# A gated Mamba and mixture-of-experts block on one core: gate folded into the output weights, residual made a sequence ahead, moments by aggregation, and a new slot table

## The chip, the cores and the metric

The kernel is one program on one core of a Trainium2 chip. The time is device microseconds of that core for one launch, as the median of repeated runs. A chip core has a matrix engine (TensorE, in the profile PE), a vector engine (VectorE, DVE), an activation engine (ScalarE, ACT), a general engine (GpSimd, POOL) and a queue engine (SyncE, SP), which here issues all transfers. Each engine takes its own instructions in the order of the program and waits on semaphores for the others.

## The reference, cut to what matters

```python
h = layernorm(x) * (1 + ca) + sa                # ca, sa, ga, cb, sb, gb: rows of silu(c) @ wmod, one per sequence
xn = (h - mean(h)) * rsqrt(var(h) + 1e-5) * norm_g + norm_b
x = x + ga * (h + mamba_fwd(xn) + mamba_bwd(xn))
h = layernorm(x) * (1 + cb) + sb
x = x + gb * moe(h)                             # 8 experts, top 2 by a router, and a shared one
# mamba: u, z = xn @ Win.T; u = silu(conv4(u)); dt = softplus(...); then for each of 16 states n
#   state = exp(dt*A[n]) * state + dt*u*B[n];  y += state*C[n]   (a scan over 512 tokens)
# y = (y + u*D) * silu(z);  result y @ Wout.T
```

Sixteen sequences of 512 tokens and 128 channels; the Mamba part has 256 inner channels (two halves of 128 partitions) and runs in both directions; every expert has 256 hidden channels. All is float32.

## The kernel before

There is a pass for each sequence `b`, and each pass has 32 **slots**: slots 0 to 15 are the 16 states of the forward scan, slots 16 to 31 those of the backward scan. Passes 2 to 14 are a hardware loop, the others are written out. Into the slots of pass `b` the kernel puts, engine by engine, the experts of sequence `b-1` (`ffn_side`, `expert_up`, `expert_silu`, `expert_sum`) and the preparation of the backward scan of `b` and of the forward scan of `b+1` (`prep`, with the slot offsets `U_AT` to `V_AT`, and `norms`). The tables of slots at the top of the file thus fix the order of every engine's queue; nothing is scheduled while the program runs.

In every slot the same five things happen. POOL makes `bt` (two halves at once) for the *next* slot (`bmul(step)`, which waits until the scan of two steps earlier is done: `bt` has two buffers). ACT makes the two halves of `psA = exp(dt*A)` for the next slot (`exps`), a half as soon as DVE has read that half of `psA` out. DVE scans both halves in place (`scan`) and multiplies them by C into `g` (`read_out`). PE adds `g` up in `psY` (`sum_y`).

Where the experts are up, a slot also has: two matmuls into `F0` and `F1` (`expert_up`), on ACT `tf` = tanh of `F0` and a copy `gf` of `F1`, on DVE in the following slot `pf` between the two read-outs, on POOL `act`; and on PE half of a down projection (`DOWN_SLOTS`), and after each second half on DVE a `facc` sum of four pieces. `up_at(slot)` and `down_at(slot)` turn a slot into a piece of expert work.

The chain to the experts of a sequence starts with the gated result of the Mamba part: the projection into `F2` (PE, `PROJ_SLOT` and the next), its sum with the kept `h` on DVE (`fx`, `FX_SLOT`), on POOL times the gate and plus a second copy of x (`x2`, two tensor operations), then layernorm (`LN3_SLOT`: four `BN_STATS` on DVE, `moments` on POOL, four activations `zF` on ACT), a transposition and the modulation into `h2T` (`H2T_SLOT`), the router's matmul (`GATE_SLOT`) and its small operations on DVE one slot later (`gate`), then `ge` (ACT), `gs` (POOL), `gw` (DVE) and `expert_weights` (POOL).

Softplus needs a logarithm, and twice in a pass (`ln1p`, in slots 9 and 28) ACT loads another table for it, and with the next function that isn't in that table it loads the first one back.

The order of parts within one slot of ACT's queue is this, and that of POOL is alike (`bmul`, `side`, `ffn_side`):

```python
exps(STEPS * b + nxt, b, nxt // N, nxt % N)   # for the next slot
ln1p(...)                                     # slots 9 and 28
s.activation(h1K, z1, ACT.Copy)               # one slot
ffn_side(b - 1, slot)                         # zF, h2T, ge, tf, gf, first facc
side(b, slot, True, b + 1)                    # norms and prep
```

Of the kernel before, what the change touches and what calls it, by code (L numbers as in the profile page):

```python
# [1163 lines left out]
```

## Time and profile before

| | us |
|---|---|
| median of 3 runs (2624.6 to 2626.51) | 2625.07 |
| the profiled execution | 2627.43 |
| its span, first to last instruction | 2625.6 |

The profiled execution took 2.36 us more than the median of the runs, and 1.83 us of it lie outside its span. Its mean granted TensorE clock is 0.897 of full speed. Times in rows are from the span's start. Two rows of one engine that follow each other overlap by some 0.05 to 0.09 us, so that what an instruction costs its queue is the distance of the starts.

### The profile page before, as it was taken

Reading aid. Unit: us, or ns where it says so; the run is one execution under the profiler, and the core shown is the slowest. Engines: PE = TensorE matmul, PEld = TensorE weight load, DVE = VectorE, ACT = ScalarE, POOL = GpSimd, SP = SyncE. Lnnn points to the kernel's source line nnn. Section 1 sums busy time; section 2 is a strip of 40 time slices with the busy share of each in tenths; the row PEclk is TensorE's granted clock in tenths of the full one; section 3 lists DMA queues with packets and bytes.
Section 4 is the critical chain, followed back from the end, with each engine's and each line's share of the span. In section 5 each row is a group of like instructions: output and inputs, shape, how many; then the busy total and the mean of one; then the engine's idle time right before and its main releaser. Section 6 shows DMA issues by size and latency. Waiting matters only on the chain. (4 is left out here: it accounts for less than half of the span.)

```text
span 2625.6 us, 37957 instructions
## 1 busy us (share of the span) xinstructions
PE 2125.2 (81%) x9893; PEld 1356.4 (52%) x9893; DVE 2288.6 (87%) x3603; ACT 1513.2 (58%) x2468; POOL 1958.1 (75%) x1437
## 2 busy tenths in 40 slices
PE   3677887978788797888889788787978879798868
PEld 1244554555555455555546555454555545455544
DVE  1699998989899898998989899898989989899973
ACT  2546656655565665656656565665556566565633
POOL 1577878778787877878777787877878787787854
PEclk6777998989899898998989899898989989899999
DMA  2334232333323233332333423333332333333320
GB/s 81 128 129 140 99 131 104 113 122 108 134 96 128 106 113 121 112 128 99 113 121 117 133 96 129 105 109 125 109 133 97 124 110 113 121 112 123 113 67 5
DMA packets 120494, 293.33 MB, mean 112 GB/s; under 512 B 18516, under 2 KB 53172, under 8 KB 120388
## 3 DMA queue, kind: packets, MB, share of 16 engines
q1 hardware_dynamic: 120388, 292.30, 33.0%
q14 instruction: 86, 0.70, 0.1%
q8 instruction: 20, 0.33, 0.0%
HBM read 285.91 MB, written 6.34 MB: 111 GB/s over the span
## 5 line engine op out<-in xcount | busy, mean ns | idle before, releaser
L426 POOL TENSOR_TENSOR bt<-v,bb 128x1024 f32<-128x1024 f32 x512 | 1207.1, 2361 | 178.2 <-DVE psA L783 175.7
L783 DVE TENSOR_TENSOR_SCAN psA<-psA,bt 128x512 f32<-128x512 f32 x1024 | 1198.0, 1216 | 126.1 <-POOL bt L426 90.9
L600 ACT ACTIVATE psA<-dt,aneg 128x512 f32<-128x512 f32 x1024 | 684.7, 688 | 745.1 <-DVE g L793 738.8
L983 PEld LDWEIGHTS psY<-ident,g 128*128 128x128 f32 x4096 | 517.4, 152 | 475.2 <-DVE g L793 267.7
L983 PE MATMUL psY<-ident,g 128*128 128x128 f32 x4096 | 606.9, 294 | 164.5 <-DVE g L793 164.4
L793 DVE TENSOR_TENSOR g<-psA,cb 128x512 f32<-128x512 f32 x1024 | 673.3, 677 | 0.0
L526 POOL TENSOR_TENSOR act<-pf,gf 128x512 f32<-128x512 f32 x288 | 366.2, 1272 | 256.5 <-DVE pf L878 224.9
L1064 PE MATMUL F<-h2T,w 128*128 128x512 f32 x576 | 337.2, 669 | 87.5 <-DVE pf L878 87.4
L1108 PE MATMUL F<-w,act 128*128 128x128 f32 x2304 | 319.4, 284 | 47.0 <-POOL act L526 43.4
L1108 PEld LDWEIGHTS F<-w,act 128*128 128x128 f32 x2304 | 291.6, 198 | 64.9 <-issue 57.9
L1067 PE MATMUL F<-h2T,w 128*128 128x512 f32 x576 | 308.3, 618 | 0.0
L878 DVE SCALAR_TENSOR_TENSOR pf<-tf,F 128x512 f32<-128x512 f32 x288 | 194.6, 676 | 73.0 <-ACT tf L693 73.0
L999 PE MATMUL psP<-xnT,wcT 128*128 128x512 f32 x512 | 248.8, 609 | 5.2 <-DVE zs L819 2.2
L693 ACT ACTIVATE tf<-F 128x512 f32<-128x512 f32 x288 | 169.7, 589 | 139.4 <-PE F L1064 138.9
L696 ACT ACTIVATE gf<-F 128x512 f32<-128x512 f32 x288 | 172.2, 598 | 73.1 <-PE F L1067 71.4
L1064 PEld LDWEIGHTS F<-h2T,w 128*128 128x128 f32 x576 | 97.8, 202 | 195.7 <-DVE pf L878 135.5
L1067 PEld LDWEIGHTS F<-h2T,w 128*128 128x128 f32 x576 | 116.8, 203 | 153.2 <-issue 152.6
L1015 PE MATMUL psP<-xnT,wzT 128*128 128x512 f32 x128 | 101.7, 888 | 91.3 <-DVE zs L819 87.6
L892 DVE SCALAR_TENSOR_TENSOR facc<-F,wts,facc 128x128 f32<-128x128 f32 x512 | 143.2, 343 | 10.7 <-PE F L1108 10.5
L999 PEld LDWEIGHTS psP<-xnT,wcT 128*128 128x128 f32 x512 | 90.8, 198 | 74.1 <-issue 65.8
L472 POOL TENSOR_TENSOR dt<-xb,ab 128x1024 f32<-128x1024 f32 x32 | 75.1, 2347 | 47.4 <-ACT ab L648 46.6
L1012 PE MATMUL psP<-xd,wdtT 8*128 8x512 f32 x128 | 93.5, 818 | 15.5 <-ACT xd L630 9.9
(134 smaller groups left out, 1730.1 us busy)
## 6 DMA issues: line engine op xcount, KB each, us to landing
bb<-bc_rows SPq DMA_DIRECT2D x256, 512.0 KB, 3.7
cb<-bc_rows SPq DMA_DIRECT2D x256, 512.0 KB, 3.6
x<-in_L_attn_x SPq DMA_DIRECT2D x16, 256.0 KB, 3.7
xR<-in_L_attn_x SPq DMA_DIRECT2D x16, 256.0 KB, 3.5
out_x<-osb SPq DMA_DIRECT2D x16, 256.0 KB, 3.9
w<-in_L_ffn_ew SPq DMA_DIRECT2D x2, 1024.0 KB
modA<-mod_table SPq DMA_DIRECT2D x16, 128.0 KB, 3.9
bc_rows<-xd SPq DMA_DIRECT2D x32, 64.0 KB, 2.8
```

The lines of the kernel that those rows point to most:

```text
L426: g.tensor_tensor(bt[:, n % 2, :, :], v[d][:, :, :], bb[:, n // 2 % 2, n % 2, :].unsqueeze(1).broadcast_to([P, NH, T]), ALU.mult).then_inc ...
L526: g.tensor_tensor(act[:, k // 2 % 3, k % 2, :], pf[:, k % 2, :], gf[:, k % 3, :], ALU.mult)\
L600: s.activation(psA[:, half * T:half * T + T], dt_[d][:, half, :], ACT.Exp, scale=aneg[d][:, half, n:n + 1]).then_inc(a_s, 1)
L696: s.activation(gf[:, k % 3, :], F1[:, :], ACT.Copy).then_inc(F1_free, 1)
L783: w.tensor_tensor_scan(ah, ah, bt[:, n % 2, half, :][:, order], 0.0, ALU.mult, ALU.add)\
L793: w.tensor_tensor(g_[:, n % 2, half, :], psA[:, half * T:half * T + T], cb[:, n // 2 % 2, n % 2, :], ALU.mult).then_inc(g_s, 1)
L878: w.scalar_tensor_tensor(pf[:, k % 2, :], tf[:, k % 2, :], 1.0, F0[:, :], ALU.add, ALU.mult).then_inc(pf_s, 1)
L983: last = m.matmul(psY[:, half * T + i * P:half * T + i * P + P], g_[:, n % 2, half, i * P:i * P + P], ident[:, :], is_transpose=True, star ...
L999: last = m.matmul(psP[:, :], wcT[d][:, half, j, :], xnT[:, lo:lo + T], start=(j == 0), stop=(j == TAPS - 1))
L1064: m.matmul(F0[:, :], w1[:, x_, half * P:half * P + P], h2T[:, :], start=True, stop=True)\
L1067: m.matmul(F1[:, :], w2[:, x_, half * P:half * P + P], h2T[:, :], start=True, stop=True)\
L1108: last = m.matmul(F2[:, i * D:i * D + D], act[:, e % 3, half, i * P:i * P + P], w3[:, ORDER[e], half, :], start=(half == 0), stop=(half == 1))
```

## The change

**The gate is folded into the output weights.** POOL multiplies both directions' output weights by the gate's row once per pass (`wg`, in `WG_SLOT` = 2), and PE projects with `wg`. The residual and the gated `h` are added ahead: `hx = h*ga + x` is made on POOL in slot 23 of the pass before, copied on ACT (`hxK`), and DVE adds it to the projection, which gives `x2` at once. POOL's two operations on `x2` and the second load of x (`xR`) fall away, `modA` has a third row, and the next load of x waits for `hx` and not for `h1`.

**Moments by aggregation.** After the four `BN_STATS` DVE waits for them, clears four numbers and does four `BN_AGGR`; POOL's `moments` has four operations in place of eight.

**A table load of its own** follows each logarithm (`preload_act_table`).

**New slots.** First norm's statistics 9 to 8, its moments 10 to 9, `z1` 11 to 10; Z pieces a slot later; `x2` 5 to 4 and its statistics in the same slot (6 before), its moments 6 to 5, `zF` 7 to 5, the transposition 8 to 6 and behind the other work of PE's slot, router 9 to 7, its small operations 10 to 8, `ge` and `gs` 11 to 9, expert weights 13 to 11. The experts' up slots begin at 7 (9 before) and leave out 9, 10 and 22; the down slots begin at 10 (12 before) and leave out 12, 13, 20 and 23.

```diff
-U_AT, XD_AT, DT_AT, LN1P_AT, Z_AT, V_AT = 0, 6, 7, 9, 9, 11
-LN_SLOT, XN_SLOT = 9, 16
+U_AT, XD_AT, DT_AT, LN1P_AT, Z_AT, V_AT = 0, 6, 7, 9, 10, 11
+STAT_SLOT, RSTD_SLOT, Z1_SLOT, H1_SLOT, STAT2_SLOT, RSTD2_SLOT, XNORM_SLOT, XN_SLOT, HX_SLOT = 8, 9, 10, 12, 13, 14, 15, 16, 23
-POSTB_SLOT, PROJ_SLOT, FX_SLOT, LN3_SLOT, H2T_SLOT, GATE_SLOT = 1, 3, 5, 6, 8, 9
+POSTB_SLOT, WG_SLOT, PROJ_SLOT, X2_SLOT, LN3_SLOT, H2T_SLOT, GATE_SLOT = 1, 2, 3, 4, 4, 6, 7
-UP_SLOTS = [slot for slot in range(9, 28) if slot not in (22,)]
-DOWN_SLOTS = [slot for slot in range(12, 32) if slot not in (19, 21)]
+UP_SLOTS = [slot for slot in range(7, 28) if slot not in (9, 10, 22)]
+DOWN_SLOTS = [slot for slot in range(10, 32) if slot not in (12, 13, 20, 23)]
...
-                wait(sp, h1_s, 2 * b)
+                wait(sp, hx_s, 2 * b)
...
-                row = mod_dram[bass.ds(b, 1), 0:2 * D].broadcast_to([P, 2 * D])
+                row = mod_dram[bass.ds(b, 1), 0:3 * D].broadcast_to([P, 3 * D])
...
-                    sp.dma_start(xR[:, :, :], t["x"][bass.ds(fb, 1)].rearrange("a (k p) d -> p (a k) d", p=P))\
-                        .then_inc(xR_in, 16)
...
-                g.tensor_tensor(stat_[:, :, 0:2], st_[:, :, 1:3], st_[:, :, 4:6], ALU.add).then_inc(sig, 1)
-                g.tensor_tensor(stat_[:, :, 2:3], st_[:, :, 1:2], st_[:, :, 4:5], ALU.subtract).then_inc(sig, 1)
+                g.tensor_tensor(stat_[:, :, 2], stat_[:, :, 1], epsilon[:, :], ALU.add).then_inc(sig, 1)
+                g.tensor_tensor(stat_[:, :, 3], stat_[:, :, 0], negative[:, :], ALU.mult).then_inc(sig, 1)
                 pool.wait_ge(sig, q + 2)
-
-                g.tensor_tensor(stat_[:, :, 0:3], stat_[:, :, 0:3], scales[:, :, :], ALU.mult).then_inc(sig, 1)
+                g.tensor_tensor(rstd_[:, :], stat_[:, :, 2], mhalf[:, :], ALU.pow).then_inc(sig, 1)
                 pool.wait_ge(sig, q + 3)
...
+                g.tensor_tensor(stat_[:, :, 4], stat_[:, :, 3], rstd_[:, :], ALU.mult).then_inc(sig, 1)
...
+                if slot == HX_SLOT:
+
+                    wait(pool, hxK_s, b)
+                    g.tensor_tensor(hx[:, :, :], z1[:, :, :], over_tiles(modA[:, 2, :]), ALU.mult).then_inc(hx_s, 1)
+                    pool.wait_ge(hx_s, 2 * b + 1)
+                    g.tensor_tensor(hx[:, :, :], hx[:, :, :], x[:, :, :], ALU.add).then_inc(hx_s, 1)
...
-                if slot == FX_SLOT:
-                    pool.wait_ge(F2_free, (DOWN + 1) * fb + PROJ + 1)
+                if slot == WG_SLOT:
                     pool.wait_ge(modF_in, 48 * fb + 48)
-                    wait(pool, o_s, 2 * fb)
-                    g.tensor_tensor(x2[:, :, :], fx[:, :, :], over_tiles(modF[:, 0, :]), ALU.mult).then_inc(x2_s, 1)
-                    pool.wait_ge(x2_s, 2 * fb + 1)
-                    pool.wait_ge(xR_in, 16 * fb + 16)
-                    g.tensor_tensor(x2[:, :, :], x2[:, :, :], xR[:, :, :], ALU.add).then_inc(x2_s, 1)
...
+                    wait(pool, F2_full, (DOWN + NE) * (fb - 1) + PROJ + 1)
+                    g.tensor_tensor(wg[:, :, :, :].rearrange("p a k d -> p (a k) d"),
+                                    wout_both[:, :, :, :].rearrange("p a k d -> p (a k) d"),
+                                    over_tiles(modF[:, 0, :]), ALU.mult).then_inc(wg_s, 1)
...
                 s.activation(ab[:, :, :], ab[:, :, :], ACT.Ln, bias=1.0).then_inc(sp_s, 1)
+                s.preload_act_table(ACT.Exp)
...
-                        if slot == FX_SLOT + 2:
+                        if slot == X2_SLOT + 2:
...
-                            s.activation(h1K[:, :, :], z1[:, :, :], ACT.Copy).then_inc(h1K_s, 1)
+                            s.activation(hxK[:, :, :], hx[:, :, :], ACT.Copy).then_inc(hxK_s, 1)
...
                 for i in range(NT):
                     w.bn_stats(st_[:, i, :], x_[:, i, :]).then_inc(sig, 1)
+                dve.wait_ge(sig, q + NT)
+                w.memset(stat_[:, :, 4], 0.0)
+                for i in range(NT):
+                    w.bn_aggr(stat_[:, i, 0:2], st_[:, i, :]).then_inc(sig, 1)
...
-                    w.tensor_tensor(fx[:, :, :], F2[:, :].rearrange("p (k c) -> p k c", c=D), h1K[:, :, :], ALU.add)\
+                    w.tensor_tensor(x2[:, :, :], F2[:, :].rearrange("p (k c) -> p k c", c=D), hxK[:, :, :], ALU.add)\
                         .then_inc(F2_free, 1)
...
+                        pe.wait_ge(wg_s, fb + 1)
...
-                                            woutT[k // NH][:, k % NH, :], start=(k == 0), stop=(k == 2 * NH - 1))
+                                            wg[:, k // NH, k % NH, :], start=(k == 0), stop=(k == 2 * NH - 1))
```

**ACT, slot 9.** Before the change, ACT's queue in the loop has here the second half of the exponentials for slot 10 (`psA`), the logarithm behind its table load (L648), and then the load that belongs to the first tanh of the experts, `tf`:

```order
L600 ACTIVATE psA<-dt,aneg 128x512
L647 REGISTER_ALU
L648 ACT_TABLE_LOAD
L648 ACTIVATE ab<-ab 128x1024
L691 ISA
L273 REGISTER_ALU
L693 ACT_TABLE_LOAD
L693 ACTIVATE tf<-F 128x512
L273 REGISTER_ALU
L696 ACTIVATE gf<-F 128x512
```

After the change the same place reads:

```order
L593 ACTIVATE psA<-dt,aneg 128x512
L640 REGISTER_ALU
L641 ACT_TABLE_LOAD
L641 ACTIVATE ab<-ab 128x1024
L642 ACT_TABLE_LOAD
L680 REGISTER_ALU
L681 ACTIVATE ge<-gd 128x4
L275 ISA
L593 ACTIVATE psA<-dt,aneg 128x512
```

The load back stands directly behind the logarithm (L642), `tf` has left the slot, and the router's exponential `ge` (L681) now stands behind both loads; before, it stood in slot 11.

**POOL, slots 9 to 11.** Before the change POOL's queue around `gs`, the operation that needs `ge`, is this; the `bt` ahead of `v` is the one for slot 11, made in POOL's slot 10, with `gs` in its slot 11:

```order
L472 TENSOR_TENSOR dt<-xb,ab 128x1024
L522 ISA
L273 REGISTER_ALU
L526 TENSOR_TENSOR act<-pf,gf 128x512
L273 ISA
L426 TENSOR_TENSOR bt<-v,bb 128x1024
L475 REGISTER_ALU
L273 ISA
L477 TENSOR_TENSOR v<-u,dt 128x1024
L504 TENSOR_TENSOR gs<-ge,ones 128x4
```

After the change:

```order
L436 TENSOR_TENSOR stat<-stat,rstd 128x4
L499 TENSOR_TENSOR gs<-ge,ones 128x4
L515 REGISTER_ALU
L519 TENSOR_TENSOR act<-pf,gf 128x512
L275 ISA
L424 TENSOR_TENSOR bt<-v,bb 128x1024
L465 ISA
L466 ISA
L467 TENSOR_TENSOR dt<-xb,ab 128x1024
L275 ISA
L424 TENSOR_TENSOR bt<-v,bb 128x1024
```

`gs` has moved two slots forward, and what stands behind it now is the second `act` of the experts, the `bt` of slot 11 (the first `bt` of this piece), `dt` and the `bt` of slot 12.

**DVE, slots 4 and 5.** Before the change, the slot of the projection's sum is slot 5, and its statistics come a slot later:

```order
L793 TENSOR_TENSOR g<-psA,cb 128x512 x2
L812 REGISTER_ALU
L819 SCALAR_TENSOR_TENSOR u<-th,psP 128x512
L900 REGISTER_ALU
L273 REGISTER_ALU
L903 TENSOR_TENSOR fx<-F,h1K 128x512
L779 REGISTER_ALU
L781 ISA
```

After the change, slot 4 has:

```order
L787 TENSOR_TENSOR g<-psA,cb 128x512 x2
L898 REGISTER_ALU
L275 REGISTER_ALU
L901 TENSOR_TENSOR x<-F,hxK 128x512
L904 ISA
L275 REGISTER_ALU
L793 BN_STATS stF<-x 128x6 x4
L794 ISA
L795 MEMSET statF 128x4
L797 BN_AGGR statF<-stF 128x2 x4
```

The sum, here written to x2 (`x` in the row), its statistics and the aggregation now stand together in slot 4, behind the read-outs `g`.

## Rows read from the trace of the kernel before

**Rows 1.** The page's part 1: engine, busy us, share, instructions.

```profile
PE 2125.2 (81%) x9893; PEld 1356.4 (52%) x9893; DVE 2288.6 (87%) x3603; ACT 1513.2 (58%) x2468; POOL 1958.1 (75%) x1437
```

**Rows 2.** Timeline of DVE from slot 4: start, us, instruction, [idle before <-releaser].

```profile
1165.68 2.35 DVE L783 TENSOR_TENSOR_SCAN psA<-psA,bt 128x512 f32<-128x512 f32 x2 [0.17 <-ACT psA L600]
...
1169.36 2.35 DVE L783 TENSOR_TENSOR_SCAN psA<-psA,bt 128x512 f32<-128x512 f32 x2 [0.16 <-ACT psA L600]
...
1174.00 2.34 DVE L783 TENSOR_TENSOR_SCAN psA<-psA,bt 128x512 f32<-128x512 f32 x2
...
1177.43 0.86 DVE L799 BATCH_NORM_STATS2 stF<-x 128x6 f32<-128x128 f32 x4
1179.46 2.35 DVE L783 TENSOR_TENSOR_SCAN psA<-psA,bt 128x512 f32<-128x512 f32 x2 [1.17 <-POOL bt L426]
...
1184.64 2.35 DVE L783 TENSOR_TENSOR_SCAN psA<-psA,bt 128x512 f32<-128x512 f32 x2 [1.65 <-POOL bt L426]
```

**Rows 3.** Timeline of DVE, slots 10, 11 and the start of 16.

```profile
1198.20 0.69 DVE L878 SCALAR_TENSOR_TENSOR pf<-tf,F 128x512 f32<-128x512 f32 x1 [2.75 <-ACT tf L693]
...
1200.33 0.36 DVE L849 MAX8 top<-gl 128x8 f32<-128x8 f32 x4
...
1202.01 2.35 DVE L783 TENSOR_TENSOR_SCAN psA<-psA,bt 128x512 f32<-128x512 f32 x2
...
1228.04 1.23 DVE L783 TENSOR_TENSOR_SCAN psA<-psA,bt 128x512 f32<-128x512 f32 x1 [0.90 <-POOL bt L426]
```

**Rows 4.** Timeline of ACT, slot 9.

```profile
1191.29 1.30 ACT L600 ACTIVATE psA<-dt,aneg 128x512 f32<-128x512 f32 x2
1192.61 1.28 ACT L648 ACT_TABLE_LOAD   x1
1193.90 1.06 ACT L648 ACTIVATE ab<-ab 128x1024 f32<-128x1024 f32 x1
1196.19 1.28 ACT L693 ACT_TABLE_LOAD   x1 [1.23 <-PE F L1064]
```

**Rows 5.** Timeline of POOL, layernorm moments in slot 6.

```profile
1179.29 0.21 POOL L433 TENSOR_TENSOR statF<-stF 128x8 f32<-128x8 f32 x1
...
1180.88 1.02 POOL L445 TENSOR_TENSOR rstdF<-statF,mhalf 128x4 f32<-128x4 f32 x1
...
1182.14 2.37 POOL L426 TENSOR_TENSOR bt<-v,bb 128x1024 f32<-128x1024 f32 x1
```

**Rows 6.** Timeline of POOL, slots 11 to 13.

```profile
1207.06 0.20 POOL L504 TENSOR_TENSOR gs<-ge,ones 128x4 f32<-128x4 f32 x1 [2.12 <-ACT ge L687]
...
1208.46 2.37 POOL L426 TENSOR_TENSOR bt<-v,bb 128x1024 f32<-128x1024 f32 x1
1210.78 1.28 POOL L461 TENSOR_TENSOR xn<-z,modA 128x512 f32<-128x512 f32 x1
...
1216.93 0.19 POOL L492 TENSOR_TENSOR gw<-gw,ge 128x4 f32<-128x4 f32 x1
```

**Rows 7.** Timeline of SP, the gate's rows being fetched.

```profile
1158.55 0.38 SPq L383 DMA_DIRECT2D modC<-mod_table  x1
```

**Rows 8.** DMA issues: KB each, median us from issue to landing.

```profile
modC<-mod_table SPq DMA_DIRECT2D x16, 1.0 KB, 3.4
```

**Rows 9.** Timeline of PE, projection in slots 3 and 4.

```profile
1162.14 2.05 PE L1081 MATMUL F<-woutT,acc 128*128 128x128 f32 x16 [0.54 <-DVE acc L837]
...
1166.62 1.95 PE L1081 MATMUL F<-woutT,acc 128*128 128x128 f32 x16
```

**Rows 10.** Timeline of PE, first and second pair into F0.

```profile
1194.19 1.90 PE L1064 MATMUL F<-h2T,w 128*128 128x512 f32 x2
...
1201.10 1.02 PE L1064 MATMUL F<-h2T,w 128*128 128x512 f32 x2
```

**Rows 11.** Busy times in one stretch: length, engines, PEclk, DMA share, GB/s.

```profile
1178.90:1192.30 13.40, 10.29 (x32) 6.46 (x33) 11.02 (x15) 9.74 (x18) 11.35 (x13) 0.50 0.33 123
```

**Rows 12.** Timeline of DVE, slot 29.

```profile
1293.70 0.69 DVE L819 SCALAR_TENSOR_TENSOR zs<-th,psP 128x512 f32<-128x512 f32 x1 [1.37 <-ACT th L621]
```

More of the change, by code:

```diff
@@ L98, in adaln_mamba_moe @@
         wdtT = [sb(f"wdtT{d}", [R, NH, P]) for d in range(2)]
-        woutT = [sb(f"woutT{d}", [P, NH, D]) for d in range(2)]
+        wout_both = sb("woutT", [P, 2, NH, D])
+        woutT = [wout_both[:, d, :, :] for d in range(2)]
         norm = sb("norm", [P, 2])
@@ L111, in adaln_mamba_moe @@
         gabs = sb("gabs", [NB, 2, D])
-        modA = sb("modA", [P, 2, D])
+        modA = sb("modA", [P, 3, D])
         modF = sb("modF", [P, 2, D])
@@ L222, in adaln_mamba_moe @@
         h1_s = sem("h1_s")
-        h1K_s = sem("h1K_s")
+        hx_s = sem("hx_s")
+        hxK_s = sem("hxK_s")
+        wg_s = sem("wg_s")
         pP_full = sem("pP_full")
@@ L412, in _ @@
             g.memset(ones[:, :], 1.0).then_inc(const_ok, 1)
-            for k, scale in enumerate((-0.5, 1.0 / D, 0.5)):
-                g.memset(scales[:, :, k:k + 1], scale).then_inc(const_ok, 1)
+            g.memset(negative[:, :], -1.0).then_inc(const_ok, 1)
             def over_tiles(row):
@@ L463, in norms @@
                     g.tensor_tensor(z1[:, :, :], xn[:, :, :], over_tiles(modA[:, 0, :]), ALU.add).then_inc(h1_s, 1)
-                if slot == LN_SLOT + 5:
-                    pool.wait_ge(lnA, 8 * b + 8)
-                    moments(st, stat, rstd, rstdA, 16 * b + 8)
+                if slot == HX_SLOT:
[3 more added lines that the diff above has]
+                    g.tensor_tensor(hx[:, :, :], hx[:, :, :], x[:, :, :], ALU.add).then_inc(hx_s, 1)
+                if slot == RSTD2_SLOT:
+                    pool.wait_ge(lnA, 16 * b + 16)
+                    moments(stat, rstd, rstdA, 8 * b + 4)
             def make_dt(b, d):
@@ L898, in ffn_side @@
                     gate_y(fb, 1, slot - POSTB_SLOT)
-                if slot == FX_SLOT:
+                if slot == X2_SLOT:
                     dve.wait_ge(F2_full, (DOWN + NE) * fb + PROJ + 1)
-                    dve.wait_ge(h1K_s, fb + 1)
+                    dve.wait_ge(hxK_s, fb + 1)
                     wait(dve, o_s, 2 * fb)
-                    w.tensor_tensor(fx[:, :, :], F2[:, :].rearrange("p (k c) -> p k c", c=D), h1K[:, :, :], ALU.add)\
+                    w.tensor_tensor(x2[:, :, :], F2[:, :].rearrange("p (k c) -> p k c", c=D), hxK[:, :, :], ALU.add)\
                         .then_inc(F2_free, 1)
                 if slot == LN3_SLOT:
-                    dve.wait_ge(x2_s, 2 * fb + 2)
-                    wait(dve, rstdF_s, 8 * fb)
-                    statistics(x2, stF, lnF)
+                    dve.wait_ge(F2_free, (DOWN + 1) * fb + PROJ + 1)
+                    wait(dve, rstdF_s, 4 * fb)
+                    statistics(x2, stF, statF, lnF, 8 * fb)
                 if slot == GATE_SLOT + 1:
@@ L1056, in expert_up @@
                 free = (DOWN + 1) * fb
+                if slot == H2T_SLOT:
+                    pe.wait_ge(zF_s, NT * fb + NT)
+                    pe.wait_ge(F2_free, free + H2T)
+                    for i in range(NT):
+                        last = m.transpose(F2[:, i * P:i * P + P], zF[:, i, :], ident[:, :])
+                    last.then_inc(F2_full, 1)
                 k = up_at(slot)
@@ L1081, in ffn_late @@
                             last = m.matmul(F2[:, i * D:i * D + D], yg[k // NH][:, k % NH, i * P:i * P + P],
-                                            woutT[k // NH][:, k % NH, :], start=(k == 0), stop=(k == 2 * NH - 1))
+                                            wg[:, k // NH, k % NH, :], start=(k == 0), stop=(k == 2 * NH - 1))
                     if slot == PROJ_SLOT + 1:
                         last.then_inc(F2_full, 1)
-                if slot == H2T_SLOT:
-                    pe.wait_ge(zF_s, NT * fb + NT)
-                    pe.wait_ge(F2_free, free + H2T)
-                    for i in range(NT):
-                        last = m.transpose(F2[:, i * P:i * P + P], zF[:, i, :], ident[:, :])
-                    last.then_inc(F2_full, 1)
                 if slot == GATE_SLOT:
```

68 lines of the change are left out of this document (29 added, 39 removed).

## Prediction

> **What bounds the kernel now.** The page comes first: DVE is busy for 87% of the span [rows 1], more than any other engine, so the question in each place is what DVE waits for. I then read DVE's timeline over one pass of the loop, a slot at a time, from the scan of slot 4 at 1165.68 to that of slot 16 at 1228.04 [rows 2, 3]: 62.36 us. The reader is to see three kinds of slot. A bare one takes 3.68 us, of which some 0.2 is a wait for the exponentials (1165.68 to 1169.36). One with a further 128x512 operation hides that wait: slot 5 has two, `u` and `fx`, and takes 4.64. I take 3.45 for the scans and read-outs alone and 0.60 for each addition. The third kind waits for something else: 1.17 and 1.65 us for `bt` at the starts of slots 7 and 8 [rows 2], 2.75 for `tf` in slot 10, 0.90 for `bt` at the start of slot 16 [rows 3]. The first two are the `x2` chain on POOL. The 2.75 is ACT's: a logarithm behind a table load, a wait for `F0`, a second load [rows 4].
>
> **From slot 4 to DVE's first read-out of slot 9.** I call the end of that read-out T, since ACT's exponentials for slot 10 start there. Before, slot 9 starts 3.68+4.64+5.46+5.18+3.68 = 22.64 after slot 4 (the slots' lengths in rows 2; the last is a bare one), and scans and a read-out take 2.85, so T is at 25.5. The edits move it so:
> - `x2` now follows in slot 4 directly on the projection, which waits for `wg`, and `wg` for the gate's rows. These are issued at 1158.55 and land 3.4 later [rows 7, 8], at 1162.0, and a 128x512 operation on POOL takes 1.28 [rows 6]: PE starts near 1163.4, not 1162.14 [rows 9]. PE is busy from there to the end of the second part (1166.62+1.95 = 1168.57), so that ends near 1169.8, some 0.6 behind DVE's read-outs (1165.68+3.45): +0.6. POOL stands for these rows with the `bt` of slot 4 behind it; it ends at 1163.3+2.37 = 1165.7, just in time, cost nothing, and if a transfer takes 1 us longer, 1 us.
> - `fx` and `x2` are one operation either way; 0.
> - Aggregation is in no row. The bounds: four small operations in 0.36 us [MAX8, rows 3] below, four BN_STATS in 0.86 [rows 2] above. A BN_AGGR reads six numbers, so it is nearest MAX8. With the clearing and a wait for its own statistics I take 0.45, twice before T: +0.9 (0.7 to 1.9).
> - The statistics of x come into slot 8 from slot 9, where they stood behind T: +0.8 [0.86 less an overlap, rows 2].
> - The router's small operations come into slot 8 from slot 10: from 0.33 before MAX8 at 1200.33 to 1202.01 [rows 3], +2.0.
> - The first `pf` comes into slot 8: +0.6.
> - The waits for `bt` at slots 7 and 8 go, since POOL has nothing more to do to `x2`: -2.95 (with what surrounds them in the slot's lengths). Moments take POOL 2.85 us [rows 5]; with four of the small operations gone, at some 0.28 each, 1.75. They lie under slots that POOL has room in.
>
> The sum is +1.95, T at 27.4, if `tf` is there in time. Now the clock. Here the granted clock is 0.50, the 1.2 GHz level, for 13.4 us [rows 11], after slots in which PE had little to do, and a pair into `F0` takes 1.90 in place of 1.02 [rows 10]. I count the new chain: `x2` summed near 4.7 after slot 4's start, statistics to 5.9, moments to 7.7, exponentials, `zF` by 11.9, transposition to 13.4, `h2T` to 15.5, then router, a DT piece and the pair into `F0`: `tf` ends near 19.0 at the 2.4 GHz level, in time for the read-out at 20.2; at the 1.2 GHz level each of the three takes 0.9 more, `tf` ends near 21.7, and DVE waits 1.6. The gf, DT and second pair behind it then make ACT late for the exponentials of slot 10 by another 0.8. The stretch lies where the clock is low now, and its gaps on PE are much the same, so I take the low level: T is in effect at 29.8.
>
> **From T to the scan of slot 16.** In slot 9 `ge` now stands behind two table loads and the logarithm. The second half of the exponentials ends at T+1.9. Load, logarithm, load take 1.29+1.08+1.28 = 3.65 [rows 4], `ge` some 0.25: `gs` starts on POOL at T+5.9. It and `act` take 1.40 [1207.06 to 1208.46, rows 6], and only then does POOL make the `bt` of slot 11, 2.31 long: the scan of slot 11 starts at T+9.8. Free of this it would be T+1.2+3.7 = T+4.9. So the wait for `tf`, 2.75, is gone and one of 4.9 for `bt` takes its place. What is queued behind on POOL is not hidden either, as these slots have the most POOL work of the pass. From T+9.6: `dt` 2.3, `bt` 2.3, `v` 2.3, expert weights 1.0 (five small ones), `bt` 2.3, then the two of the modulation, `act` and `bt` 6.15 [1210.78 to 1216.93, rows 6], `act` and `bt` 3.55, moments 1.75, `act` and `bt` 3.55: T+34.8. The last slot being DVE's own, the scan of slot 16 starts at T+35.2.
>
> So slot 16 starts at 65.0 (62.6 if the clock holds), against 62.36 before.
>
> ACT's exponentials end at 1192.59 and the load starts at 1192.61, the logarithm 0.01 after the load's end [rows 4]: a switch costs its 1.28 and nothing else. The Trainium skill (ScalarE: Activation LUTs, "What ACT_TABLE_LOAD costs") says that a switch of table costs 1283 ns and then about 1380 ns of draining. The load's duration agrees with the row, the drain doesn't. By the row load, logarithm and load take 3.65; by the skill's figure they would take 6.4 and `ge` come 2.8 later.
>
> **From slot 16 to the next slot 4.** The down slots shift by one, so that `facc` leaves slot 23, which has no `pf` and where it hid the wait for exponentials: +0.25. In slot 29 the wait of 1.37 for a tanh behind the table load [rows 12] goes, as Z comes a slot later; the exponentials of slot 30 now start behind both loads and cost 0.6: -0.8. `hx` on POOL in slot 23 is two operations of 1.28 [rows 6] in a slot without `act`, after slots in which POOL waits for DVE; 0, and if that room is gone, up to 2.5. The third row of `modA` and the missing load of x concern transfers that have a pass's time; 0. Together -0.55.
>
> **Sum.** A pass of the loop: 65.0-62.36-0.55 = +2.1. Fifteen passes have both experts and scans: +31. The ends: in the last pass `x2` loses POOL's two operations (2.6) and moments 1.1, and gains 0.45; the first passes lose moments twice and a tanh ahead of the logarithm, some 2.5: -6 in all. 2627.4+25 = 2652 for a profiled execution, whose time now is 2.4 above the median: 2650.
>
> **The rivals.**
> - *PE's clock holds through slots 6 to 8* (the case on the other side). For it: PE is busy almost without a gap from the transposition on, where before it waited. Against it: 13.4 us at 0.50 in the same slots now [rows 11]. Price: 2.4 us a pass less, a pass at -0.3, the whole 2627.4-5-6, as a median 2614. It decides at `tf`: ready before DVE's first read-out of slot 8, or not.
> - *The clock is low again after slot 9.* PE has only `sum_y` to do while POOL waits for `ge`. If it stays low until the third pair into `F0`, behind the down projection, Z and `sum_y`, `pf` in slot 12 waits up to 3 us: +45, 2695. Against it: DVE is late there too, and I count some 0.3 us in hand even with part of it low.
> - *POOL isn't held by `ge`.* Then the 4.9 goes and with it the queue behind, some 6.5 a pass: 2650-97 = 2553. Against it stands the order of both queues; nothing in the rows speaks for it.
> - *The second load drains ACT first.* Nothing stands between the logarithm and the load now, where before ACT waited for `F0`; if the load back had to wait for the logarithm's results as long as that runs, 1.06 [rows 4], and the first load for the exponentials likewise, `ge` and all behind it came 2.1 later: times 15, 2682. Against it stands the first load, directly behind the exponentials. By the Trainium skill's figure for the drain (ScalarE: Activation LUTs, the same section) it would be 2692.
>
> **How the numbers follow.** Forecast (low clock in slots 6 to 8, held by `ge`): 0.58, its own range 2632 to 2672 from aggregation up to 0.5 each dearer and the exponentials 0 to 1.7 late. Clock holds: 0.20. Low again: 0.12. Not held: 0.08. Drain: 0.02. The range of 2606 to 2688 leaves out "not held" and most of "low again". Within 0.2% (5 us, about what a measurement of this kernel can tell from no change): 0.12, half from the forecast's low end and half from the clock's. Faster 0.24: 0.08, 0.14 of the clock's and 0.02 of the forecast's. Slower 0.64.
>
> **What would show it.** In the profile after: `psA` in slot 11 waiting 4 to 5 us for `bt`, that `bt` behind `gs`, and `gs` waiting for `ge`; ACT with load, logarithm and load in one piece of 3.65; no `bt` wait at slots 7 and 8; four BN_AGGR within 0.3 to 0.5; PE's first projection waiting for `wg`; `pf` in slot 8 waiting 1.6 for `tf` with the granted clock at 0.50. If that clock stands at 1.00 there, or the wait at slot 11 is under 3 us, the forecast is too high; if PE is at 0.50 through slots 10 to 12 and `pf` waits in slot 12, too low.

## The result, and the profile after

The changed kernel takes 2667.16 us (median of 4 runs, 2662.65 to 2671.37), beside 2625.28 us for the kernel before on the same chip: a ratio of 1.0158, 95% interval 1.0145 to 1.0172. It is slower by 1.6%, 17 us above the predicted 2650 and inside the range. The profiled execution took 2671.37 us, 43.94 more than the one of before. One execution of the first experiment below (8637.84 us) and one of the second (3090.94) were slow ones; the medians given there include them, the ratios don't.

The page's part 1 (busy us, share, instructions) and groups of its part 5:

```profile
PE 2119.8 (79%) x9893; PEld 1351.9 (51%) x9893; DVE 2309.6 (87%) x3843; ACT 1508.7 (57%) x2468; POOL 1936.3 (73%) x1259
...
L777 DVE TENSOR_TENSOR_SCAN psA<-psA,bt 128x512 f32<-128x512 f32 x1024 | 1198.7, 1217 | 164.8 <-POOL bt L424 86.3
...
L890 DVE SCALAR_TENSOR_TENSOR facc<-F,wts,facc 128x128 f32<-128x128 f32 x512 | 143.6, 346 | 26.0 <-PE F L1107 26.0
```

DVE is busy 21 us longer than in [rows 1], with 240 more instructions: the clearing and the aggregation. The rest is waiting. The page's totals don't say where, so the timeline is read again, slot by slot. This is DVE in one pass, from slot 8 to slot 12:

```profile
1198.06 0.68 DVE L876 SCALAR_TENSOR_TENSOR pf<-tf,F 128x512 f32<-128x512 f32 x1
...
1199.25 0.86 DVE L793 BATCH_NORM_STATS2 st<-x 128x6 f32<-128x128 f32 x4
1200.16 0.17 DVE L797 BATCH_NORM_AGGREGATE stat<-st 128x2 f32<-128x6 f32 x1
1200.19 0.06 DVE L795 MEMSET stat<- 128x4 f32 x1
1200.25 0.28 DVE L797 BATCH_NORM_AGGREGATE stat<-st 128x2 f32<-128x6 f32 x3
1200.45 0.16 DVE L843 COPY gl<-F 128x32 f32<-128x32 f32 x1
...
1202.43 2.35 DVE L777 TENSOR_TENSOR_SCAN psA<-psA,bt 128x512 f32<-128x512 f32 x2
...
1211.56 0.18 DVE L867 RECIPROCAL gw<-gs 128x4 f32<-128x4 f32 x1 [1.25 <-POOL gs L499]
1215.20 2.34 DVE L777 TENSOR_TENSOR_SCAN psA<-psA,bt 128x512 f32<-128x512 f32 x2 [3.47 <-POOL bt L424]
```

ACT in slot 9 and 10, and POOL behind it:

```profile
1207.38 1.28 ACT L641 ACT_TABLE_LOAD   x1
1208.67 1.06 ACT L641 ACTIVATE ab<-ab 128x1024 f32<-128x1024 f32 x1
1209.75 1.28 ACT L642 ACT_TABLE_LOAD   x1
1211.04 0.21 ACT L681 ACTIVATE ge<-gd 128x4 f32<-128x4 f32 x1
```
```profile
1211.32 0.20 POOL L499 TENSOR_TENSOR gs<-ge,ones 128x4 f32<-128x4 f32 x1 [7.18 <-ACT ge L681]
1211.50 1.26 POOL L519 TENSOR_TENSOR act<-pf,gf 128x512 f32<-128x512 f32 x1
1212.72 2.36 POOL L424 TENSOR_TENSOR bt<-v,bb 128x1024 f32<-128x1024 f32 x1
```

The hold is there as forecast: `ge` behind load, logarithm and load, `gs` behind `ge`, `act` and `bt` behind `gs`, and DVE idle for 1.25 and then 3.47, together 4.72 us. In [rows 3] the same stretch has 2.75 for `tf`, which is gone: `pf` at 1198.06 follows its read-out directly. What wasn't forecast is at the end of the pass. PE first, then DVE, from slot 30 to the next pass's slot 0:

```profile
1311.97 2.08 PE L1013 MATMUL psP<-xnT,wzT 128*128 128x512 f32 x2 [3.38 <-DVE zs L817]
1313.83 1.91 PE L981 MATMUL psY<-ident,g 128*128 128x128 f32 x8
1315.54 1.64 PE L1107 MATMUL F<-w,act 128*128 128x128 f32 x8
```
```profile
1317.32 1.13 DVE L890 SCALAR_TENSOR_TENSOR facc<-F,wts,facc 128x128 f32<-128x128 f32 x4 [1.38 <-PE F L1107]
1320.50 2.35 DVE L777 TENSOR_TENSOR_SCAN psA<-psA,bt 128x512 f32<-128x512 f32 x2 [2.06 <-issue]
```

The kernel before, DVE in the same place:

```profile
1302.80 1.12 DVE L892 SCALAR_TENSOR_TENSOR facc<-F,wts,facc 128x128 f32<-128x128 f32 x4
1305.08 2.35 DVE L783 TENSOR_TENSOR_SCAN psA<-psA,bt 128x512 f32<-128x512 f32 x2 [1.17 <-POOL bt L426]
```

A piece of Z now stands in slot 30. It waits 3.38 us for `zs`, PE does nothing meanwhile, and Z, `sum_y` and the last down projection then run near the 1.2 GHz level (2.08 for a pair that took 1.02 elsewhere; the granted clock is the third number from the end of this row, behind the busy times of the engines):

```profile
1310.00:1317.00 7.00, 5.03 (x18) 3.89 (x19) 5.94 (x9) 3.21 (x5) 6.83 (x4) 0.52 0.29 95
```

`facc` waits 1.38 for them, and the next pass's first scan starts 2.06 after `facc`, a stretch for which the trace names no releaser. In the kernel before, the same piece stands one slot earlier and has the same wait, but there a whole slot lies between it and the last `facc`, which doesn't wait:

```profile
1294.44 1.63 PE L1015 MATMUL psP<-xnT,wzT 128*128 128x512 f32 x2 [3.82 <-DVE zs L819]
```

I measured the slots of the 13 passes of the loop from the third on and took means, in us (the starts of the scans in DVE's timeline):

| stretch | before | after | difference | forecast |
|---|---|---|---|---|
| scan of slot 0 to slot 4 | 16.42 | 16.67 | +0.25 | in the -0.55 |
| slot 4 to slot 16 | 62.40 | 63.12 | +0.72 | +2.6 |
| slot 16 to slot 31 | 71.32 | 70.42 | -0.90 | in the -0.55 |
| slot 31 to the next slot 0 | 5.72 | 8.45 | +2.73 | 0 |
| a pass | 155.85 | 158.66 | +2.81 | +2.1 |

The 2.73 at the end of a pass are three things: the addition `zs`, which now stands in slot 31 (0.6), the wait of `facc` (0.96 in the mean, 0 before) and a longer idle stretch ahead of slot 0's scan (2.25 for 1.17). That stretch comes with the loop's way back: the passes before the loop end without one, and so does the thirteenth, behind which the program goes straight on into a written-out one; there slot 31 to slot 0 takes 4.5 before and 5.8 after.

The thirteen make 36.4 of the 43.94. The pass before them has +3.1, the last one with scans +8.5, and the rest (start, first pass, tail) -3.6+0.75-1.1 = -4.0: together 44.0.

### The profile page after: what moved, and what is told of

It is laid out like the page before. It is cut to its first block and busy times, and to the rows that moved or that the text cites. A ratio compares the mean times of both kernels' runs of the same rounds, so it can differ in the third digit from the quotient of the medians.

```text
span 2669.6 us, 37830 instructions
## 1 busy us (share of the span) xinstructions
PE 2119.8 (79%) x9893; PEld 1351.9 (51%) x9893; DVE 2309.6 (87%) x3843; ACT 1508.7 (57%) x2468; POOL 1936.3 (73%) x1259
## 5 line engine op out<-in xcount | busy, mean ns | idle before, releaser
L981 PEld LDWEIGHTS psY<-ident,g 128*128 128x128 f32 x4096 | 524.0, 153 | 448.6 <-DVE g L787 224.9
L1068 PE MATMUL F<-h2T,w 128*128 128x512 f32 x576 | 335.0, 665 | 105.9 <-DVE pf L876 104.4
L1107 PE MATMUL F<-w,act 128*128 128x128 f32 x2304 | 329.1, 289 | 106.8 <-POOL act L519 99.7
L1107 PEld LDWEIGHTS F<-w,act 128*128 128x128 f32 x2304 | 301.6, 204 | 122.9 <-issue 95.0
L1071 PE MATMUL F<-h2T,w 128*128 128x512 f32 x576 | 317.4, 635 | 0.0
L1013 PE MATMUL psP<-xnT,wzT 128*128 128x512 f32 x128 | 100.0, 875 | 64.2 <-DVE zs L817 62.7
L614 ACT ACTIVATE th<-psP 128x512 f32<-128x512 f32 x128 | 76.2, 596 | 77.9 <-PE psP L1013 75.8
```

Of the source, the lines that this page charges most:

```text
L981: last = m.matmul(psY[:, half * T + i * P:half * T + i * P + P], g_[:, n % 2, half, i * P:i * P + P], ident[:, :], is_transpose=True, star ...
L1068: m.matmul(F0[:, :], w1[:, x_, half * P:half * P + P], h2T[:, :], start=True, stop=True)\
L1071: m.matmul(F1[:, :], w2[:, x_, half * P:half * P + P], h2T[:, :], start=True, stop=True)\
L1107: last = m.matmul(F2[:, i * D:i * D + D], act[:, e % 3, half, i * P:i * P + P], w3[:, ORDER[e], half, :], start=(half == 0), stop=(half == 1))
```

## The experiments

All ratios are to the kernel before, run on the same chip. Places are given by slots, since each kernel runs at its own times.

**`ge` ahead of the loads.** The computation is unchanged; ACT issues `ge` in slot 9 before the first table load.

```diff
-                if slot == GATE_SLOT + 2:
-                    act_e.wait_ge(gate_s, GATES * fb + GATE_D)
-                    s.activation(ge[:, :], gd[:, :], ACT.Exp).then_inc(ge_s, 1)
...
+                    if ffn and slot == GATE_SLOT + 2:
+                        act_e.wait_ge(gate_s, GATES * (b - 1) + GATE_D)
+                        s.activation(ge[:, :], gd[:, :], ACT.Exp).then_inc(ge_s, 1)
```

> The changed kernel with one thing moved: in ACT's slot 9 the router's exponential ge stands ahead of the logarithm and its two table loads, not behind them. Theory (POOL is held by ge): gs starts some 3.6 us earlier, the wait of 3.5 us for bt at the start of slot 11 falls to under 1 us, and what is queued behind on POOL comes as much earlier; about 3.5 us a pass, so about 2613 us. Rival (the loss is spread over aggregation, fold and the start of a pass, and POOL's hold is made good by slack later): under 1 us a pass, above 2650 us.

Measured: 2608.37 us, 0.9935 (0.9915 to 0.9955), 5 us below what the theory had. ACT and the scan of slot 11:

```profile
1185.03 0.19 ACT L713 ACTIVATE ge<-gd 128x4 f32<-128x4 f32 x1
1185.24 1.28 ACT L641 ACT_TABLE_LOAD   x1
```
```profile
1189.63 2.35 DVE L777 TENSOR_TENSOR_SCAN psA<-psA,bt 128x512 f32<-128x512 f32 x2 [1.75 <-ACT psA L593]
```

The releaser changes from POOL's `bt` to ACT's exponentials, which the loads hold in either kernel, and 1.75 is left of 4.72. Slot 4 to slot 16 takes 59.24 in place of 63.12. The one edit is worth 59 us of the whole: the hold is the largest single cost of the change, and it comes from the order of two things on ACT.

**`ge` two slots later.** `ge` and `gs` in slot 11, the reciprocal in 12, the weights in 13, so that no one waits for `ge`.

```diff
-                if slot == GATE_SLOT + 2:
+                if slot == GATE_SLOT + 4:
```

> The changed kernel with the router's tail back where it was: ge and gs in slot 11, gw in 12, expert weights in 13 (9, 9, 10, 11 in the changed kernel). Theory (POOL is held): the hold goes altogether, and what is left at the start of slot 11 is a wait for ACT's exponentials behind both loads, some 1.7 us; 2600 to 2615 us. Rival (spread): above 2650 us.

Measured: 2624.51 us, 0.9994 (0.9981 to 1.0008), 10 to 25 us above what was expected. Slot 11 has no wait for `bt`, but slot 12 has new ones. PE, DVE and the granted clock (PEclk) there:

```profile
1198.59 2.08 PE L1013 MATMUL psP<-xnT,wzT 128*128 128x512 f32 x2 [4.27 <-DVE zs L817]
1200.45 1.57 PE L1068 MATMUL F<-h2T,w 128*128 128x512 f32 x2
```
```profile
1202.69 0.69 DVE L876 SCALAR_TENSOR_TENSOR pf<-tf,F 128x512 f32<-128x512 f32 x1 [1.32 <-ACT tf L687]
```
```profile
1194.00:1198.00 4.00, 0.32 (x3) 0.12 (x2) 3.58 (x5) 3.67 (x8) 4.00 (x3) 1.00 0.26 95
1198.00:1204.00 6.00, 5.41 (x15) 2.89 (x16) 4.66 (x6) 2.48 (x7) 5.92 (x5) 0.72 0.45 152
```

PE has 0.32 us of work in 4 us, and then runs at 0.72 of its clock. Slot 12 takes 7.27 in the mean of the thirteen passes, 5.63 in the changed kernel, and five of them have a long slot 9, where the changed kernel has three. This is the rival "low again after slot 9": it exists, in a kernel where DVE is early enough to meet it. In the changed kernel `pf` in slot 12 waits in none of the thirteen passes; that DVE, held by `bt`, simply comes later there than PE is my reading of the rows.

**The old slots, the rest of the change kept** (the gate folded into the weights, aggregation, the extra preload; U and Z, norms, router and experts where they stood before; only the statistics of `x2` stand a slot earlier than then, in slot 5 behind the sum):

```diff
-U_AT, XD_AT, DT_AT, LN1P_AT, Z_AT, V_AT = 0, 6, 7, 9, 10, 11
+U_AT, XD_AT, DT_AT, LN1P_AT, Z_AT, V_AT = 0, 6, 7, 9, 9, 11
-POSTB_SLOT, WG_SLOT, PROJ_SLOT, X2_SLOT, LN3_SLOT, H2T_SLOT, GATE_SLOT = 1, 2, 3, 4, 4, 6, 7
+POSTB_SLOT, WG_SLOT, PROJ_SLOT, X2_SLOT, LN3_SLOT, H2T_SLOT, GATE_SLOT = 1, 2, 3, 5, 5, 8, 9
...
```

> Fold, residual ahead, aggregation and the extra table load as changed, but with the slots of before (x2 in slot 5 with its statistics behind it, transposition 8, router 9, experts up from 9, down from 12, Z as before). Theory (the slots cost, the rest gains): the bt waits at slots 7 and 8 are gone (-2.9 us a pass), the wait for tf is 1.3 us shorter, aggregation costs up to 1.35: 2580 to 2600 us. Rival (the fold and aggregation themselves cost): above 2625 us.

Measured: 2600.11 us, 0.9901 (0.9885 to 0.9918), the upper end of what the theory gave.

**Aggregation alone, in the kernel before** (statistics closed by BN_AGGR on DVE, four small operations fewer on POOL):

```diff
+                dve.wait_ge(sig, q + NT)
+                w.memset(stat_[:, :, 4], 0.0)
+                for i in range(NT):
+                    w.bn_aggr(stat_[:, i, 0:2], st_[:, i, :]).then_inc(sig, 1)
```

> The kernel before with aggregation alone: after each four BN_STATS DVE waits, clears and does four BN_AGGR, POOL's moments have four operations in place of eight. Theory (aggregation is cheap, 0.45 us each, and POOL's shorter moments pay for it where DVE waits for bt): 2600 to 2625 us. On the start of a pass in the loop: if DVE's longer loop body is what makes the idle time before slot 0 longer (1.2 us before, 2.3 after the change), it is above 2 us here too; if it is the late down projection or Z's shift, it stays at 1.2 us. Rival (aggregation costs 1 us each or more): above 2640 us.

Measured: 2608.65 us, 0.9934 (0.9918 to 0.9951). So aggregation alone makes the kernel 16 us faster. The folded gate, with what comes along with it, gives another 9, and the new slots cost 67. The 9 can't be put down to the gate alone: the preload is in that difference too. Here the load back waits 1.2 to 1.5 us for `F0`; in the old slots with the preload it waits for nothing, and the wait for `tf` is 2.05 in place of the 2.60 here. No run parts the two.

```profile
1180.65 2.35 DVE L771 TENSOR_TENSOR_SCAN psA<-psA,bt 128x512 f32<-128x512 f32 x2 [1.10 <-ACT psA L588]
...
1190.77 0.69 DVE L870 SCALAR_TENSOR_TENSOR pf<-tf,F 128x512 f32<-128x512 f32 x1 [2.60 <-ACT tf L681]
```

The two kernels take 5.68 and 5.65 from slot 31 to slot 0, as before, so the 2.73 at the end of the pass comes with the new slots, and not with the number of instructions in the loop.

**Z of the forward direction back a slot, in the changed kernel.** The piece in slot 30 then stands in slot 29.

```diff
-                if k - Z_AT in (0, 1):
-                    open_piece(Z, k - Z_AT)
+                if k - Z_AT + (d == 0) in (0, 1):
+                    open_piece(Z, k - Z_AT + (d == 0))
...
```

> The changed kernel with the two Z pieces of the forward preparation back in slots 28 and 29 (their sums on DVE in 29 and 30); those of the backward one stay. Theory: the late Z piece is what makes the end of a loop pass dear. PE stands for the sum of slot 30, its next down projection comes late, facc waits in slot 31, and the branch back, which otherwise starts while DVE still works, starts late too. Then slot 31 to the next slot 0 goes back from 8.45 to 5.7 us, slot 29 costs 1.5 more again: about -1.2 us a pass, 2649 us. Rival (DVE's longer loop body or the other edits make the branch back dear): slot 31 stays above 7.5 us and the kernel at 2665 us or above.

Measured: 2666.32 us, 1.0156 (1.014 to 1.0173): no gain where 18 us were expected. The end of the pass does what the theory says: 5.77 from slot 31 to slot 0 (2.68 less) and 6.53 in slot 29 (1.54 more, [rows 12]). But slot 4 to slot 16 takes 64.28, 1.16 more: `x2` waits 1.0 for PE in slot 4 in the mean (0.3 in the changed kernel), and 6 of the 13 passes have a long slot 9 (5.8 to 5.9), where the changed kernel has 3. One of the four passes with the long wait for `x2`, PE and DVE:

```profile
385.15 3.40 PE L1086 MATMUL F<-wg,acc 128*128 128x128 f32 x16 [2.04 <-POOL wg L505]
```
```profile
393.33 0.69 DVE L901 TENSOR_TENSOR x<-F,hxK 128x512 f32<-128x512 f32 x1 [2.36 <-PE F L1086]
```

The first half of the projection takes 3.40 here, at a granted clock of 0.65, and 2.02 at 1.00 in the pass behind it, where `x2` waits 0.32. PE has stood 2 us for `wg` before it, since POOL waits some 4 us for the gate's rows in every pass. So the cause of the 2.73 is shown, and the saving is given back in stretches that no edit touched, where the granted clock falls at other moments.

**PE kept busy in slot 30.** Three further matmuls ahead of that piece of Z, into F0, whose results nothing reads.

```diff
+                if d == 0 and k == Z_AT + 1:
+                    wait(pe, pf_s, 2 * NE * (b - 1))
+                    for _ in range(3):
+                        m.matmul(F0[:, :], wzT[d][:, 0, :], xnT[:, PAD:PAD + T], start=True, stop=True)
```

> The changed kernel with three matmuls more (128x512, into F0, which nobody reads then) on PE in slot 30, where it stands for DVE's sum. They compute nothing that is used. Theory (a low clock makes the down projection late): the granted clock stays at 1.00 there, the wait of facc in slot 31 falls from 1.0 us to under 0.3, and the time from slot 31 to slot 0 from 8.45 to some 7.3 us: 2650 us. Rival (the order of PE's queue alone makes it late): the wait stays at 1.0 us or grows, 2667 us or more.

Measured: 2649.34 us, 1.0098 (1.0079 to 1.0117), as expected: more work on PE takes 18 us away. The four executions lie between 2639.85 and 2655.72, and the profiled one is the fastest of them. PE, DVE and the clock:

```profile
1296.24 2.74 PE L1014 MATMUL F<-xnT,wzT 128*128 128x512 f32 x6
1299.78 1.13 PE L1017 MATMUL psP<-xnT,wzT 128*128 128x512 f32 x2 [0.80 <-DVE zs L817]
```
```profile
1303.67 1.12 DVE L890 SCALAR_TENSOR_TENSOR facc<-F,wts,facc 128x128 f32<-128x128 f32 x4
1306.55 2.35 DVE L777 TENSOR_TENSOR_SCAN psA<-psA,bt 128x512 f32<-128x512 f32 x2 [1.75 <-issue]
```
```profile
1298.00:1305.00 7.00, 6.20 (x32) 3.84 (x31) 6.79 (x12) 4.20 (x7) 6.83 (x4) 1.00 0.30 105
```

Z takes 1.13 in place of 2.08, the clock is 1.00, and `facc` no longer waits. Slot 31 to slot 0 is 6.55. So 1.9 of the 2.73 is PE at its lower level. Of the other 0.8, 0.6 is `zs`, which still stands in slot 31, and 0.2 stays in the stretch before slot 0's scan (1.41 in the mean, 1.17 in the kernel before); the cause of this last piece is open.

**Both, `ge` first and Z back.**

> Both single edits together: ge ahead of the logarithm, and the forward Z pieces back. If the two losses lie apart they add up: 2608 us less some 18, 2590 us. If the queue of POOL takes back what the end of the pass gives: 2605 us.

Measured: 2605.62 us, 0.9915 (0.9888 to 0.9942). Beside 2608.37 for `ge` first alone: the two don't add up, and the time is the 2605 that was given for that case. The end of the pass takes 2.9 less than with `ge` first alone, slots 16 to 31 take 1.7 more (nearly all of it slot 29), slots 4 to 16 0.7 more.

**The extra table load taken out** of the changed kernel (the preload that stands behind each logarithm):

```diff
-                s.preload_act_table(ACT.Exp)
```

> The changed kernel without the extra table load behind the logarithm: the load back then comes with ge in slot 9 and with the exponentials in slot 29. Theory (the load back is needed at the same place either way): within 5 us of the changed kernel, 2662 to 2672 us. Rival (the extra load costs or hides something of its own): more than 10 us away.

Measured: 2673.72 us, 1.0177 (1.016 to 1.0194), 6.6 us more than the changed kernel, whose interval it touches, and 1.7 above the expected stretch; a pass takes 158.61 for 158.66, with the same waits. The preload adds no load: every one of these kernels has 65 of them. Whether it is asked for or comes by itself with the next exponential makes next to no difference in these slots, so asking for it isn't what costs in the hold, its place ahead of `ge` is.

**PE kept busy in slots 5 and 7** of the changed kernel (three and one such matmuls), to lift the clock before the first pair into F0.

> The changed kernel with four matmuls more on PE (128x512, into F0, which nobody reads then, nothing used): three at the end of slot 5, where PE stands for DVE, and one in slot 7 after the sum. In the changed kernel 3 of the 13 loop passes lose some 1.8 us more in slot 9 than the others, with the clock at the lower level near 33 us into the pass, and the last pass with scans loses 4.3 us there. Theory (that is the clock): these go, worth 0.5 us a pass and 3 to 4 us once: 2653 to 2660 us. Rival (the order of the queues makes them, not the clock): 2665 us or more, as PE only has more to do.

Measured: 2665.46 us, 1.0157 (1.0118 to 1.0196), where 2653 to 2660 was expected. In the profiled execution the long slot 9 is gone from all 13 passes (4.04 to 4.54), slot 9 is 0.37 shorter in the mean, and the last pass with scans is 3.7 shorter, all as expected; but the second pass is 1.9 longer and what follows the last scans 3.7. The four executions spread from 2658.11 to 2679.54, so four can't show or rule out a gain of 5 us. And it isn't certain that the edit does what it is for: with the same matmuls in the next run, two of thirteen passes have a long slot 9 again.

**`ge` first, with PE kept busy** in slots 30, 5 and 7:

> ge ahead of the logarithm, and the fillers of both places (three matmuls in slot 30, three in slot 5, one in slot 7). The sum of the single edits: 2608 less 18 for slot 30 and less some 8 for the early ones: 2580 to 2590 us. If the fillers hold up something else once POOL is free: 2605 us.

Measured: 2593.38 us, 0.9876 (0.9857 to 0.9894), 3 us above the expected stretch. It is the fastest of all: 34 us below the kernel before on its chip and 74 below the changed one. A pass takes 153.5, slot 4 to slot 16 59.10, slot 31 to slot 0 6.96. Two passes have a slot 9 of 5.76 and 5.89, the granted clock being 0.78 in the 7.2 us from slot 7 of the first of them on.

**The old slots, with PE kept busy** in slots 5 to 8 (seven such matmuls):

```diff
+                        fill(b - 1, {5: 2, 6: 2, 7: 2}.get(slot, 0))
...
+                        fill(b - 1, {8: 1}.get(slot, 0))
```

> Fold, residual ahead and aggregation with the slots of before, and fillers on PE in slots 5, 6 and 7 (two each, at the end) and 8 (one). With the slots of before PE is at the lower level through slots 7 to 10, and DVE waits 2.0 us for tf in slot 10. Theory (the clock makes tf late): the wait falls to under 1 us; 2600 us less 15 to 25. Rival (the logarithm and its load on ACT make tf late, PE's pair was there in time): the wait stays above 1.5 us and the kernel at 2597 to 2603 us.

Measured: 2630.68 us, 1.0012 (1.0002 to 1.0022): 30 us more than without them, where 15 to 25 less was expected. PE, ACT and DVE around slot 9:

```profile
1342.49 3.78 PE L1056 MATMUL F<-xnT,wzT 128*128 128x512 f32 x4
...
1349.96 0.66 PE L1065 MATMUL F<-ident,zF 128*128 128x128 f32 x4
```
```profile
1350.74 0.78 ACT L677 ACTIVATE h2T<-F,modC 128x512 f32<-128x512 f32 x1 [4.59 <-PE F L1065]
```
```profile
1353.81 2.35 DVE L777 TENSOR_TENSOR_SCAN psA<-psA,bt 128x512 f32<-128x512 f32 x2 [3.30 <-ACT psA L593]
...
1358.78 0.69 DVE L876 SCALAR_TENSOR_TENSOR pf<-tf,F 128x512 f32<-128x512 f32 x1 [2.05 <-ACT tf L687]
```

And DVE in the old slots without them:

```profile
1338.14 2.35 DVE L777 TENSOR_TENSOR_SCAN psA<-psA,bt 128x512 f32<-128x512 f32 x2 [0.79 <-ACT psA L593]
...
1343.11 0.69 DVE L876 SCALAR_TENSOR_TENSOR pf<-tf,F 128x512 f32<-128x512 f32 x1 [2.05 <-ACT tf L687]
```

The added work stands in PE's queue ahead of the transposition for the router (1349.96), at the lower level too (3.78 for two, each recorded as two). The transposition starts 8.1 us after the scan of slot 8, without them 4.9, so `h2T` is late, the exponentials behind it on ACT are late, and the scan of slot 10 waits 2.5 more. And the wait for `tf` is 2.05 in both, as the rival had it: `tf` starts directly behind the second table load in both, so what held it was ACT's queue and not PE's clock. That rival gave 2597 to 2603 us; neither side had seen that the added work holds up `h2T`.

## Why the prediction was right or wrong

The forecast had the sign and, within 17 us, the size. Its main mechanism, POOL held by `ge`, is shown by the run with `ge` first. But two of its terms were wrong on opposite sides, by some -1.9 and +2.1 us a pass, and that they nearly cancel is luck. Of the 19 us by which the profiled execution misses the sum, 9 are in the loop's thirteen passes, 6 in the last pass with scans, and the rest at the start and the end.

- *POOL held by `ge`*: right in place and size. `gs` starts 6.0 after T (forecast 5.9), the scan of slot 11 at T+9.9 (9.8), with 4.72 of waiting for a forecast 4.9. Slot 16 comes at T+36.5, 1.3 later than the 35.2: slots 12 to 14 wait 0.5, 0.9 and 0.8 for `bt`, and my sum for the queue behind the hold was that much short.
- *The waits for `bt` in slots 7 and 8 go*: right; slots 6 and 7 take 3.68 each.
- *`x2` waits for the gate's rows, +0.6*: right in kind. In the passes of the loop the rows land 11.5 to 12.9 us after slot 0's start, POOL stands 3.2 to 4.6 for them, PE up to 1.65 for `wg`, and `x2` waits 0 to 0.7 for the projection, 0.3 in the mean.
- *Aggregation at 0.45 each*: right. From the end of the four BN_STATS (1199.25+0.86) to the next operation's start at 1200.45 it is 0.34. Without it that operation would start some 0.09 before the recorded end, as DVE's operations do elsewhere (two read-outs 0.60 apart last 0.68), so the price is 0.43.
- *The clock in slots 6 to 8*: this step failed, where the prediction said "The stretch lies where the clock is low now, and its gaps on PE are much the same, so I take the low level". The gaps are not the same. In the stretch of [rows 11] PE waits four times, once 0.6 us and three times 1.5 to 1.6; in the changed kernel it waits once, 2.85 us, and then works from 1186.80 to 1192.8 without a wait. The granted clock of the changed kernel, from 25.9 us after the pass's start on:

```profile
1186.90:1190.30 3.40, 3.40 (x11) 1.65 (x12) 3.40 (x5) 2.75 (x6) 1.71 (x1) 0.52 0.48 152
1190.30:1200.80 10.50, 8.90 (x40) 4.86 (x39) 10.09 (x23) 8.19 (x14) 6.62 (x4) 0.99 0.45 157
1200.80:1207.60 6.80, 5.44 (x20) 2.78 (x18) 6.41 (x24) 4.46 (x9) 3.19 (x5) 0.76 0.01 4
...
1354.30:1357.70 3.40, 3.40 (x4) 1.28 (x5) 3.27 (x5) 0.90 (x2) 0.82 (x1) 0.50 0.80 261
```

  In [rows 11] it is 0.50 for 13.4 us; here it is back at 0.99 when `h2T`, router and the first pair run, and `pf` waits for nothing. T comes at 26.9 in this pass; the sum had 27.4, and the choice of the low level made it 29.8. The last row is another pass, one of three in thirteen in which the low level falls on the first pair. PE and DVE in it:

```profile
1354.23 2.03 PE L1068 MATMUL F<-h2T,w 128*128 128x512 f32 x2
```
```profile
1367.37 2.35 DVE L777 TENSOR_TENSOR_SCAN psA<-psA,bt 128x512 f32<-128x512 f32 x2 [1.77 <-ACT psA L593]
```

  Those three passes take 64.2 from slot 4 to slot 16 and the other ten 62.8, where I had 65.0 and 62.6. So both sums were near, and I chose the wrong case for ten passes of thirteen. The three didn't come about as I had it either: `pf` in slot 8 waits only 0.13 to 0.26 for `tf`, not 1.6, as router and DT piece ahead of the pair ran at or near full clock (1.06 and 1.12 to 1.20), and the exponentials of slot 10 are 1.7 to 1.8 late, not 0.8. The rival "PE's clock holds" is what happened in this stretch; its time of 2614 didn't come, since the pass lost elsewhere.
- *From slot 16 to the next slot 4, -0.55*: slots 0 to 4 and 16 to 31 give -0.65, with slot 29 at 4.98 in place of 6.53. But the term left the last slot out, where +2.73 stands. 0.6 of it is only `zs`, which left slot 29 for it (I had -0.8 there, and it is -1.55). The other 2.1 come from the piece of Z in slot 30, which PE reaches after a wait of 3.4, with the last `facc` close behind. I had costed Z's new slot for ACT (the tanh behind the load) and not for PE, its clock and the `facc` behind it. This is the largest error, and it hid the one before.
- *The ends, -6*: the start, the first pass and the tail give -4.0. The last pass with scans, which I counted as one of fifteen like the others, costs 8.5. In the kernel before it waits less than the others (1.89 for `tf`); in the changed one `x2` waits in slot 4 for the projection, and the exponentials of slot 10 are late:

```profile
2453.69 0.69 DVE L901 TENSOR_TENSOR x<-F,hxK 128x512 f32<-128x512 f32 x1 [2.14 <-PE F L1086]
...
2480.37 2.35 DVE L777 TENSOR_TENSOR_SCAN psA<-psA,bt 128x512 f32<-128x512 f32 x2 [2.43 <-ACT psA L593]
```

- *The second load drains ACT first*: no. The load at 1209.75 starts 0.02 after the logarithm's end, and `ge` 0.01 after the load's. The drain that the Trainium skill gives (ScalarE: Activation LUTs, "What ACT_TABLE_LOAD costs") isn't seen here either; its 1283 ns for the load agree.
- *POOL isn't held*: no, by the rows above.

What stays open is which of PE's waits decides its clock in slots 6 to 8, why the stretch ahead of slot 0's scan, on the loop's way back, grows from 1.17 to 2.25 when `facc` is late (1.41 with PE at full clock, 1.23 with Z a slot back), and why the passes of the same kernel differ: the low level falls at other moments in them, and the experiments moved it without a rule that I could show.

## What to carry to other kernels

Cost a moved step on every engine that it touches, the one that only supplies it too: here Z's new slot was worked out for ACT, and what it cost was PE's. When a small operation on one engine gates a large one on another, look at what stands ahead of it in its queue: 0.2 us of work ahead of two table loads, not behind them, is worth 59 us of this kernel. And matmuls that only keep PE busy paid here where PE was the last releaser of a wait and had run dry before (slot 30, 18 us). Where it mainly showed a low clock, no gain could be measured, and where they stood ahead of work that another engine waits for they cost 30 us.

## What the runs showed that I hadn't expected

The granted clock decides between two timings of the same code. In one execution of the changed kernel the twelve passes that the loop goes back from take 157.1 to 160.9 us (the thirteenth 155.0), and slot 9 is 4.0 to 4.6 or 5.9 long as the low level falls beside or on one pair of matmuls. With Z a slot back, 2.7 us were saved at the end of a pass and 1.5 paid in slot 29, both as expected from the rows, and a further 1.2 was lost between slots 4 and 16, which the edit didn't touch. With smaller gains elsewhere 0.5 us of a pass was left, and nothing of it can be told in the median. An edit's worth, read in its own slots, isn't its worth in the whole.
